# Graph attention with experts: edges from the clamped last row are counted, not gathered; degree counts get a PSUM bank of their own

## What is computed

```python
h = (x_flat @ W_gat).reshape(M, HEADS, NUM_EXPERTS)          # M = 6250, HEADS = 4, NUM_EXPERTS = 4
loops = jnp.arange(M)
src = jnp.concatenate([edge_index[0], loops])                # 131072 edges, both ends drawn from 0..8191
dst = jnp.concatenate([edge_index[1], loops])
e = leaky_relu(a_src[src] + a_dst[dst], 0.2)
e_max = segment_max(e, dst); ee = exp(e - e_max[dst])
denom = segment_sum(ee, dst)
agg = segment_sum(h[src] * alpha[:, :, None], dst) + b_gat   # alpha = ee / denom[dst]
...                                                          # layernorm, top 2 of 4 experts, softmax: the gates
for ei in range(4):                                          # experts: gelu(x @ W1 + b1) @ W2 + b2, weighted by the gate
```

## Time and profile before

| | us |
|---|---|
| median of three runs | 2700.95 |
| lowest and highest | 2700.74, 2704.62 |
| the profiled execution, its own time | 2702.96 |
| its span | 2701.3 |
| busy: PE, DVE, ACT, POOL | 2030.3, 1444.2, 759.3, 1691.1 |

### The profile page before, as it was taken

How to read it: one execution, slowest core, us unless ns; L and a number is a source line. 1 busy time by engine, 2 the same in 40 slices (tenths; PEclk the granted TensorE clock), 3 DMA queues, 4 the chain that set the end, 5 groups by cost and what they waited for, 6 DMA issues and landing times. The chain is left out here.

```text
span 2701.3 us, 31226 instructions
## 1 busy us (share of the span) xinstructions
PE 2030.3 (75%) x10560; PEld 1371.9 (51%) x10560; DVE 1444.2 (53%) x2751; ACT 759.3 (28%) x1268; POOL 1691.1 (63%) x1686
## 2 busy tenths in 40 slices
PE   2498997999999999998985999999999930000028
PEld 2355764556566666565663666666666620000016
DVE  7486775665666666654785334334334320006984
ACT  2243443334343344332452112112112100000015
POOL 0476774676676777663554777777777777774401
PEclk9699998999999999999996999999999975555559
DMA  7975567444444544443343222222222221113627
GB/s 214 290 204 166 170 183 264 131 138 136 135 142 137 143 141 138 118 125 108 113 121 91 53 52 57 55 50 56 57 49 57 56 33 17 17 17 110 208 75 324
DMA packets 273593, 320.76 MB, mean 119 GB/s; under 512 B 98721, under 2 KB 228214, under 8 KB 272408
## 3 DMA queue, kind: packets, MB, share of 16 engines
q0 software_dynamic: 68416, 133.35, 20.3%
q1 hardware_dynamic: 160552, 144.95, 17.6%
q10 hardware_dynamic: 44464, 40.43, 4.5%
HBM read 241.24 MB, written 77.32 MB: 118 GB/s over the span
## 5 line engine op out<-in xcount | busy, mean ns | idle before, releaser
L778 POOL DMA_INDIRECT c_xg<-xb_dram,src x784 | 786.6, 1003 | 356.3 <-issue 232.2
L2175 POOL DMA_INDIRECT er<-row_dram,gi x784 | 740.5, 945 | 240.3 <-issue 229.8
L2594 PE MATMUL ps_c<-eo,shift 128*128 128x256 f32 x294 | 68.1, 389 | 438.2 <-ACT shift L2558 434.6
L2253 PE MATMUL ps_em<-zT_all,ew 128*128 128x512 f32 (+1 forms) x832 | 351.6, 575 | 15.8 <-DMA eb_r<-in_eb 15.5
L2272 PE MATMUL ps_en<-ew,hid 128*128 128x256 f32 x1568 | 347.0, 379 | 0.6 <-DVE deg L2388 0.6
L2272 PEld LDWEIGHTS ps_en<-ew,hid 128*128 128x128 f32 x1568 | 297.5, 190 | 61.0 <-issue 23.2
L2318 ACT ACTIVATE hid<-ps_em,eb 128x512 f32<-128x512 f32 (+1 forms) x208 | 137.3, 663 | 569.0 <-PE ps_em L2253 568.6
L2413 DVE TENSOR_TENSOR eo<-ps_en,eb_r 128x1024 f32<-128x1024 f32 (+1 forms) x52 | 60.5, 1163 | 424.0 <-PE ps_en L2272 424.0
L2594 PEld LDWEIGHTS ps_c<-eo,shift 128*128 128x128 f32 x294 | 55.9, 194 | 450.2 <-issue 442.8
L805 PE MATMUL ps_e<-c_we,c_eaT 64*128 64x256 f32 x1568 | 227.6, 409 | 37.9 <-DVE c_xg L1134 33.4
L1134 DVE TENSOR_TENSOR c_xg<-ps_e,c_xg 128x1024 f32<-128x1024 f32 x196 | 235.2, 1216 | 11.2 <-DMA c_xg<-xb_dram,src 7.7
(11 more groups left out here) (299 smaller groups left out, 2700.9 us busy)
## 6 DMA issues: line engine op xcount, KB each, us to landing
c_eaT<-in_eaT SPq DMA_DIRECT2D x196, 128.0 KB
eo_dram<-eo ACTq DMA_DIRECT2D x48, 512.0 KB, 3.0
eo<-eo_dram SPq DMA_DIRECT2D x8, 2048.0 KB, 11.8
c_xg<-xb_dram,src POOLq DMA_INDIRECT x784
er<-row_dram,gi POOLq DMA_INDIRECT x784
c_xl<-xn_dram SPq DMA_DIRECT2D x24, 512.0 KB, 5.0
c_xm<-xm_dram SPq DMA_DIRECT2D x24, 512.0 KB, 4.4
erow<-c_none ACTq DMA_DIRECT2D x1, 10240.0 KB, 45.7
```

Of the source, the lines that this page charges most:

```text
L778: pool.indirect_dma_start(xg[:, k % NB, b, :], None, M["xb_dram"], bass.IndirectOffsetOnAxis(ap=M["src1"][:, k * B + b:k * B + b + 1], axi ...
L2175: pool.indirect_dma_start(er[:, r, b, :], None, M["row_dram"], bass.IndirectOffsetOnAxis(ap=gi[:, r, b:b + 1], axis=0)).then_inc(s_get[r], 16)
L2253: m = pe.matmul(ps_m[n % (KE - 1)][:, 0:w], w1[:, e, k, c * P:(c + 1) * P], xT[:, k, at], start=(k == 0), stop=(k == KD - 1))
```

## The change

Four things are changed.

1. `keys` adds 8192 to the destination of each edge with a source of 6249 or more (two more VectorE operations on 128 x 1024). Such edges sort behind all others. `reach` then counts only the edges below 6272 that have a source under 6249, and `FIXED` goes from 47 to 36.
2. The counting has 98 columns in place of 64: 49 for the gathered edges and 49 for the edges that read the last row (`begins` marks them; it is a second load of 512 KB, and `last_row` one of a few KB). The counts accumulate in one PSUM bank of their own, `counted`; `ps_m` has two banks in place of three. A step covers 22 columns of edges, so there are 47 steps, and the step g comes in unit g + 1. `add_degrees` is gone; one copy (`degrees`) takes all counts at the end.
3. The tail of each expert follows its 12 full units. `offsets` comes in unit 48, and the reduction over the partitions on GpSimd comes between batch 35 and batch 36, counted from 0.
4. The edges from the last row enter as one term: `own_and_last` computes its score and the node's own, `first_sums` multiplies the term by its count and starts `sums`, both on VectorE in `gat_edges_and_experts`. `attend_and_combine` doesn't set them up any more (`M["m"]` and `M["rows"]` are kept).

```diff
-FIXED = 47
+FIXED = 36
...
                         z.done(nc.vector.tensor_scalar(dst, dst, float(KEYTOP), None, ALU.add))
+                        z.done(nc.vector.tensor_scalar(clamped, src, float(N - 1), float(NBIN), ALU.is_ge, ALU.mult))
+                        z.last()
                         z.done(nc.vector.tensor_scalar(src, src, float(N - 1), None, ALU.min))
+                        z.done(nc.vector.tensor_tensor(dst, dst, clamped, ALU.add))
...
+                pool.wait_ge(s_most, 1)
+                nc.gpsimd.partition_all_reduce(M["most"][:, 1:2], M["most"][:, 0:1], P, bass.bass_isa.ReduceOp.max).then_inc(s_most, 1)
                 last = batches(pool)
                 with pool.Fori(FIXED, last) as j:
...
                 for r in range(R):
                     gather(last, r)
-                pool.wait_ge(s_most, 1)
-                nc.gpsimd.partition_all_reduce(M["most"][:, 1:2], M["most"][:, 0:1], P, bass.bass_isa.ReduceOp.max).then_inc(s_most, 1)
...
-                sp.dma_start(ends[:, :], A["ei"][1].rearrange("(p c) -> p c", p=P)).then_inc(s_ends, 16)
+                for t, x in ((ends, 1), (begins, 0)):
+                    sp.dma_start(t[:, :], A["ei"][x].rearrange("(p c) -> p c", p=P)).then_inc(s_ends, 16)
+                sp.dma_start(last_row[:, :], M["row_dram"][N - 1].partition_broadcast(P)).then_inc(s_ends, 16)
...
+                up(0)
+                for u in range(UNITS):
+                    if 0 <= u - 1 < KC:
+                        count(u - 1)
+                    if u + 1 < UNITS:
+                        e = (u + 1) // (NG + 1)
+                        if e > u // (NG + 1):
+                            pe.wait_ge(s_w[e], 48)
+                        up(u + 1)
+                    down(u)
+                    if u == AT_OFF:
+                        pe.wait_ge(s_deg, 1)
+                        pe.wait_ge(s_set, 1)
+                        pe.wait_ge(s_const, 3)
+                        pe.matmul(ps_off[:, 0:NT], lower[:, :], M["deg"][:, 0, :], start=True, stop=True)
+                        pe.matmul(ps_off[:, NT:2 * NT], ones[:, :], M["deg"][:, 0, :], start=True, stop=True).then_inc(s_off, 1)
...
                 lists()
                 spread(0)
+                spread(1)
+                for u in range(UNITS):
+                    if u % (NG + 1) == 0:
+                        dve.wait_ge(s_w[u // (NG + 1)], 48)
+                    give(u)
+                    if u >= 1 and u + 1 < KC:
+                        spread(u + 1)
+                    if u == KC:
+                        degrees()
+                    if u == AT_OFF:
+                        offsets()
+                        own_and_last()
                 dve.sem_inc(s_pace, E2 // (R * P * MB))
-                offsets()
+                first_sums()
                 dve.wait_ge(s_most, 2)
...
-                c.done(nc.vector.tensor_tensor(den[:, :, :], a, M["adst"][:, :, :], ALU.add))
...
-                c.done(nc.vector.tensor_copy(sums[:, :, 0:HC], M["rows"][:, :, HEADS:ROWC]))
-                c.done(nc.vector.memset(sums[:, :, HC:ROWC], 1.0))
-                c.last()
-                c.done(nc.vector.scalar_tensor_tensor(m[:, :, :], den[:, :, :], 0.2, den[:, :, :], ALU.mult, ALU.max))
```

More of the change, by code:

```diff
@@ L2120, in gat_edges_and_experts @@
         eo = sb("eo4", [P, 2, G, D])
[L2121 removed]
+        ps_m = [ctx.enter_context(nc.psum_tensor(f"ps_em{c}", [P, G * P], F32)) for c in range(NM)]
         cols = ctx.enter_context(nc.psum_tensor("cols4", [P, P], F32))
@@ new lines, in lists, with spread @@
+                    z.last()
+                def spread(g):
+                    b, n = g % 2, compared(g)
+                    lo = ends.bitcast(F32)
+                    at = slice(g * CT, g * CT + n)
+                    two = cols[:, :].rearrange("p (x c) -> p x c", x=2)[:, None, :, 0:NT]
+                    if g >= 2:
+                        dve.wait_ge(s_cnt, g - 1)
+                    nc.vector.tensor_tensor(hot_hi[:, b, 0:n, :].rearrange("p n (x c) -> p n x c", x=2), two.broadcast_to([P, n, 2, NT]),
+                                            hi[:, at][:, :, None, None].broadcast_to([P, n, 2, NT]), ALU.is_equal).then_inc(s_hi, 1)
+                    dve.wait_ge(s_hi, g + 1)
@@ L2405, in offsets, with own_and_last @@
                     z.last()
                     dve.sem_inc(s_most, 1)
-                def give(u, e, b, m, T):
+                def own_and_last():
+                    own, far = ex[:, :, 0, :], ex[:, :, 1, :]
+                    z.done(nc.vector.tensor_scalar(pad[:, :], M["deg"][:, 1, :], 0.5, PAD, ALU.is_lt, ALU.mult))
+                    z.done(nc.vector.tensor_tensor(own, M["rows"][:, :, 0:HEADS], M["adst"][:, :, :], ALU.add))
+                    z.done(nc.vector.tensor_tensor(far, last_row[:, None, 0:HEADS].broadcast_to([P, NT, HEADS]), M["adst"][:, :, :], ALU.add))
+                    z.last()
+                    z.done(nc.vector.scalar_tensor_tensor(ex[:, :, :, :], ex[:, :, :, :], 0.2, ex[:, :, :, :], ALU.mult, ALU.max))
+                    z.last()
+                    z.done(nc.vector.tensor_tensor(far, far, pad[:, :, None].broadcast_to([P, NT, HEADS]), ALU.add))
+                    z.last()
+                    z.done(nc.vector.tensor_tensor(M["m"][:, :, :], own, far, ALU.max))
+                    z.last()
+                    nc.vector.tensor_tensor(ex[:, :, :, :], ex[:, :, :, :], M["m"][:, :, None, :].broadcast_to([P, NT, 2, HEADS]), ALU.subtract).then_inc(s_lift, 1)
@@ new lines, in first_sums, with wide, heads @@
+                def first_sums():
+                    own, far = ex[:, :, 0, :], ex[:, :, 1, :]
+                    rows = M["rows"]
+                    part = begins[:, 0:NT * HC].bitcast(F32).rearrange("p (t c) -> p t c", c=HC)
+                    def wide(x):
+                        return x[:, :, :, None].broadcast_to([P, NT, HEADS, NE])
+                    def heads(x):
+                        return x.rearrange("p t (h c) -> p t h c", c=NE)
+                    dve.wait_ge(s_ex, 1)
+                    z.done(nc.vector.tensor_tensor(far, far, M["deg"][:, 1, :, None].broadcast_to([P, NT, HEADS]), ALU.mult))
+                    z.last()
+                    z.done(nc.vector.tensor_tensor(heads(part), last_row[:, None, HEADS:ROWC].rearrange("p o (h c) -> p o h c", c=NE).broadcast_to([P, NT, HEADS, NE]), wide(far), ALU.mult))
+                    z.done(nc.vector.tensor_tensor(heads(rows[:, :, HEADS:ROWC]), heads(rows[:, :, HEADS:ROWC]), wide(own), ALU.mult))
+                    z.done(nc.vector.tensor_tensor(rows[:, :, 0:HEADS], own, far, ALU.add))
+                    z.last()
+                    z.done(nc.vector.tensor_tensor(rows[:, :, HEADS:ROWC], rows[:, :, HEADS:ROWC], part, ALU.add))
+                    z.last()
```

210 lines of the change are left out of this document (89 added, 121 removed).

## The result

The kernel after takes 2486.05 us (median of four runs, 2485.02 to 2489.19) against 2701.02 of the kernel before in the same comparison: a ratio of 0.9203, 95% interval 0.9187 to 0.9219. The forecast was 2488.0. Its profiled execution took 2486.78, 216.2 less than that of before, with a span of 2485.1.

The account below looks back on a forecast made before the run. GpSimd's list of gathers was taken to bound the attention stage. The terms -219.8 + 6.2 - 3.4 + 1 + 0 + 2 + 1.5 - 0.5 = -213.0 us gave 2488 us for the median, range 2479 to 2503.

Parts of the forecast that it names:

- Rival B: Gathered list: the added 8192 is lost in the key, 49 batches still run, +5.8 us, 2706.8; chance 3%.
- What bounds it: Attention stage: GpSimd's list of 784 gathers, 1.249 us each, sets its length, with about 250 us of room.
- Part 1: GpSimd's gathers: 38 batches run in place of 49, 176 gathers fewer at 1.249 us each, -219.8 us.
- Part 2: GpSimd's reduction moved ahead of the last two batches: +6.2 us there, -3.4 at the stage's end, where SyncE is last.
- Part 3: GpSimd's new mid-queue wait for the largest degree (`most`, likeliest at 2182): up to 9 us, +1 taken.
- Rival A: Experts' chain decides because counting with 98 columns doesn't stream; GpSimd waits some 54 us, 2541; chance 7%.
- Part 4: Experts' chain, spreading, two `ps_m` banks and `first_sums`: hidden under GpSimd's list with some 19 us of cover, 0.
- Rival C: Experts' units: two `ps_m` banks make TensorE wait for Gelu, up to 2.8 us a unit, 2619; chance 3%.
- Part 5: Attention stage: VectorE's new work on SBUF (`lists`, `own_and_last`, `first_sums`) holds gathers, 0 to 8 us, +2 taken.
- Part 6: Other stages: two more operations in `keys`, +1.5 us; four VectorE operations gone at the last stage's start, -0.5 us.

Follow-up runs that it names:

- e1: The kernel after without the two operations on the keys, so edges from the last row stay in the gathered list (784 gathers): 2702.81 us, ratio 1.0006.
- e2: The kernel before with only the two operations on the keys and FIXED = 36 (608 gathers): 2484.37 us, ratio 0.9192.
- e7: The kernel after with reach larger by eleven batches (784 gathers), all other edits kept: 2702.29 us, ratio 1.0004.
- e5: The kernel after without GpSimd's reduction; TensorE turns the column and VectorE takes the maximum one unit later: 2476.52 us, ratio 0.9174.
- e3: The kernel after with GpSimd's reduction put back behind the last gather: 2482.73 us, ratio 0.9188.
- e9: e8 with SyncE's first stores and index loads moved ahead of the weights of experts 1 to 3: 2468.39 us, ratio 0.9138.
- e6: The kernel after with reach larger by four batches (672 gathers): 2560.30 us, ratio 0.9479.
- e8: e5 with batches of 12 gathers in place of 16 and FIXED 48 (600 gathers): 2470.84 us, ratio 0.9150.
- e4: The kernel after with the offsets one unit later (49 in place of 48), so the largest degree comes late: 2490.31 us, ratio 0.9215.
- e10: The kernel after with FIXED 35 in place of 36, so GpSimd asks for the largest degree one batch earlier: 2495.34 us (one run).
- e11: The kernel after with FIXED 28 in place of 36, so GpSimd asks for the largest degree eight batches earlier: 2635.87 us (one run).

## Why the prediction was right, step by step

Rival B is out at once: 608 gathers ran, not 784.

**What bounds it**: right. GpSimd's list of gathers set the stage, and each entry costs its time: e1, e2 and e7 show it from both sides, e5 for the reduction.

**Part 1**, -219.8: right. The batches are 38 and the gathers 608; e7 measures 220.6 for the 176.

**Part 2**: the reduction's +6.2 is right (from 2178.93 to 2185.33 are 6.4 us where 0.30 were, so +6.1, and 0.25 more on the gather behind it; taking it out gave 5.2). The -3.4 at the end is the step that failed as a mechanism: SyncE was said to be last, and it is not. Measured is -3.8, which is the reduction's 6.4 us gone from the end less a drain 2.6 longer (7.3 for 4.7). The size came right by a wrong mechanism; e3, where -2.5 was expected by the same reasoning and +1.0 came, exposed it.

**Part 3**, +1 for `most`: 0 measured. It comes at 2176.5 against a likeliest 2182, and GpSimd needs it at 2184.8. The first `give` was at 1491.83 against the 1494.9 that I took, which is 3 us of the difference. `begins` did not hold it up: `lists` started 2.6 us later against the first gather than before, but TensorE's first matmul waited for the weights until 1468.74, 10.1 us behind the first gather, where it had been 9.8 before. The counting costs what was taken:

```profile
1491.57 1.16 PE L2277 MATMUL counted<-hot_hi,hot_lo 128*128 128x98 bf16 x22
...
1492.56 0.66 PE L2288 MATMUL ps_em<-zT_all,ew 128*128 128x512 f32 x1
```

22 matmuls begin within 0.99 us, 45 ns each, against 44 taken and the 29 of the earlier trace rows at 64 columns. Rival A is out by this. (The Trainium skill, "TensorE: Matmul & The Clock Gate", Back-to-back issue gap: about 81 ns at 128 columns. This row at 98 is well under 98/128 of that, 62; the measurement decides.)

**Part 4**, 0: right. The last `give` is at 2199.18 and `mosti` at 2205.4, 20 us ahead of GpSimd's last gather. Rival C is out: over the whole stage TensorE's `up` waited 2.4 us in all for ScalarE to give back a bank, against 0.4 with three banks, and unit 48 was given 5 us early, not late. In e9 these 20 us are down to 7 (`mosti` done at 2202.1, last gather's end 2209.1): the next cut of GpSimd's list is worth little before VectorE and TensorE decide.

**Part 5**, +2: 0.5 measured. The timeline of after under `lists` and under `first_sums`:

```profile
1466.56 0.67 DVE L2366 TENSOR_SCALAR begins<-begins 128x1024 f32<-128x1024 int32 x1
1467.27 1.23 DVE L2368 SCALAR_TENSOR_TENSOR ends<-hi,ends 128x1024 f32<-128x1024 f32 x1
1467.61 0.47 SPq L2251 DMA_DIRECT2D ew<-in_eW  x1
1467.75 1.56 POOL L2199 DMA_INDIRECT er<-row_dram,gi  x1 [0.30 <-issue]
...
1469.78 2.40 DVE L2381 TENSOR_TENSOR hot_hi<-cols,hi 128x2156 bf16<-128x2156 f32 x1
...
1470.87 0.94 POOL L2199 DMA_INDIRECT er<-row_dram,gi  x1 [0.30 <-issue]
...
2202.26 0.97 DVE L2439 TENSOR_TENSOR begins<-last_row,ex 128x784 f32<-128x784 f32 x1
...
2203.06 0.98 POOL L2199 DMA_INDIRECT er<-row_dram,gi  x1 [0.30 <-issue]
```

Three gathers under `lists` take 1.06, 1.00 and 1.56 in place of 0.945, 0.8 us in all; under `own_and_last` and `first_sums` none takes more than 0.98. Before, `lists` had held two gathers as well (1.06 and 1.12, 0.3 us), so 0.5 is new. All of these, the one of 0.98 among them, have one thing in common: each began while a VectorE operation was running, and ended 0.81 to 0.86 us after that operation's end (1469.31 against 1468.50 for L2368, 2204.04 against 2203.23 for L2439). The 7.12 of the earlier trace rows is the same: it ended 0.82 after `shift`. So such an operation costs a gather roughly what is left of it when the gather begins, and a short one seldom meets that moment. But over 200 of the 608 gathers began under the operations of `spread`, and none of those took more than 0.96; what sets these operations apart is open. (The Trainium skill, "SBUF — State Buffer", the two separate sides: by its rule 4 us more were worked out. The rows of L2368 and L2439, with two SBUF inputs, agree with the rule; the 0.94 under L2381, which has two SBUF inputs as well, doesn't.)

**Part 6**, +1.5 and -0.5: not resolved. The first gather of the fourteen executions lies anywhere from 1450.9 to 1459.4, that of e1, without the two operations, in the middle at 1453.7; the last stage is 250.7 to 252.6 long, with and without the removed operations. Both effects are under what these runs can tell.

In sum 213.0 were forecast and 216.2 came in the profiled execution. By the ledger, the stretch of the gathers fell by 212.4 where parts 1, 2, 3 and 5 gave 210.6, the end by 3.8 where 3.4 was given. Ahead of the stage +1.5 was forecast and -0.8 came; in the last stage -0.5 was forecast and +0.8 came. The last two differences, +2.3 and -1.3, are within what such stages vary, so part of the closeness of the total is luck.

## What to carry to other kernels

When one queue's list sets a stage, price it per entry from start to start and cut entries: here nearly all of the gain of a change in four parts came from the two operations that shortened the list. Before saying what ends a stage, read the closing rows of each engine's queue, not only its last work. A reduction or wait placed in the middle of such a list is tied to whatever constant sets its place: 20 us too early cost 14 us, 160 us too early 154.

## What was unexpected of the hardware

- **GpSimd's closing drain went with the number of gathers, not with the code around them.** All eight kernels with 608 gathers have 7.3 us behind GpSimd's last work, with the reduction last, in the middle or absent, one, two or nine batches in the loop, and the next stage beginning anywhere from 2222.5 to 2381.6; 600 gathers give 5.0 (two kernels), 672 4.0, 784 4.7 (three). e6 and e7 have after's code with another `reach`. It isn't the wait for the last gather's data: with the reduction 6 us behind the last gather (e2, e3) the drain still ends 7.3 behind the reduction. Why is open. 608 gathers were always 38 batches, so the number of batches is not parted from that of gathers, and no run varied either by a few. e8's 2.3 us less in the drain is thus a gift.
- A gather that begins under one of VectorE's longer operations can be held until 0.81 us after that operation's end, and under other operations of the same length is not held at all (part 5).
- The 6 us ahead of a reduction lie beside a semaphore wait of the reduction itself (e4), so an early place with a wait costs the longer of the two, not both; after a real wait the next gather comes 1.2 us later besides (e4, e10, e11).
- Kernels with the same code ahead of this stage (after, e3, e4, e10 and e11) begin it at 1451.7 to 1458.6, 7 us apart; what varies there was not looked into.
